# A graph network on one Trainium2 core: the first half of x requested when both edge arrays have landed

## What is computed

```
agg = segment_sum(x[src], dst, N)                       # neighbours of every node
h   = relu(batch_norm(((1 + eps) * x + agg) @ W1 + b1))  # 512 -> 1024
h   = relu(batch_norm(h @ W2 + b2))                      # 1024 -> 512
x   = layernorm(x + x + h)
h   = relu(x @ LW1 + lb1) @ LW2 + lb2                    # 512 -> 256 -> 512
x   = layernorm(x + h + segment_sum(h[src], dst, N))
```

## Time and profile before

| | us |
|---|---|
| median of three runs (lowest, highest) | 286.44 (284.9, 287.74) |
| the profiled execution's own time | 287.6 |
| its span, first to last instruction | 285.8 |
| PE busy | 259.5 (91%) |
| VectorE busy | 144.4 (51%) |
| ScalarE busy | 123.0 (43%) |
| GpSimd busy | 76.6 (27%) |

### The profile page before, as it was taken

One profiled execution on the slowest core, in us unless ns is written; L12 is line 12 of the kernel. 1 busy time (PEld: TensorE's weight loads), 2 busy tenths in 40 slices (PEclk: granted clock), 3 DMA queues, 4 the chain that ended last, 5 costly groups with the idle time before them and its releaser, 6 DMA issues.

```text
span 285.8 us, 4044 instructions
## 1 busy us (share of the span) xinstructions
PE 259.5 (91%) x1581; PEld 221.6 (78%) x1581; DVE 144.4 (51%) x348; ACT 123.0 (43%) x217; POOL 76.6 (27%) x73
## 2 busy tenths in 40 slices
PE   0657999998999999999999999999769999999991
PEld 0636998886888888888888888888649888888770
DVE  1588997552743144444443313004474545448884
ACT  1407353424867047555556220200445445342694
POOL 5420000000920006565656700048301211112120
PEclk9999999999999999999999999999986999999998
DMA  4276000000056810000003795009000000000044
GB/s 139 93 277 240 0 2 0 2 0 6 2 203 236 274 42 1 2 0 0 2 20 126 254 234 102 0 19 202 11 1 2 1 0 2 0 0 2 3 180 175
DMA packets 21846, 20.43 MB, mean 71 GB/s; under 512 B 13911, under 2 KB 14846, under 8 KB 21826
## 3 DMA queue, kind: packets, MB, share of 16 engines
q1 hardware_dynamic: 21320, 19.91, 22.8%
q0 software_dynamic: 160, 0.13, 0.2%
q10 hardware_dynamic: 346, 0.10, 0.2%
HBM read 10.94 MB, written 5.92 MB: 59 GB/s over the span
## 4 chain that ended last, share of the span: by engine, by line
PE 81%; DVE 7%; ACT 5%; DMA 4%; issue 1%; DVEq 0%; SPq 0%; POOLq 0%
PE ps L1006 19%; PE ps L993 19%; PE ps L941 17%; PE ps L1078 7%; PE ps L1067 6%; PE ps L893 3%; PE ps L923 2%; PE ps L1052 2%; DVE hot_s L683 2%; PE ps L1125 2%; DMA src_i<-in_src 2%; PE ps L1043 1%; DMA pairs<-pair 1%; DMA run<-pairs,start_i 1%; PE ps L1064 1%
## 5 line engine op out<-in xcount | busy, mean ns | idle before, releaser
L758 DVE BATCH_NORM_STATS2 stats<-ps 128x6 f32<-128x500 f32 (+1 forms) x36 | 21.6, 599 | 63.1 <-PE ps L1006 35.2
L941 PE MATMUL ps<-AT,xh 128*128 128x500 f32 (+1 forms) x120 | 45.2, 385 | 0.0
L941 PE MATMUL ps<-AT,xl 128*128 128x500 f32 (+1 forms) x120 | 42.8, 364 | 0.0
L993 PE MATMUL ps<-h0h,wh 128*128 128x500 f32 (+1 forms) x96 | 34.0, 354 | 0.0
L993 PE MATMUL ps<-h0h,wl 128*128 128x500 f32 (+1 forms) x96 | 33.8, 352 | 0.0
L993 PE MATMUL ps<-h0l,wh 128*128 128x500 f32 (+1 forms) x96 | 33.7, 351 | 0.0
L443 ACT ACTIVATE AT<-ps 128x500 fp32r<-128x500 f32 x25 | 14.8, 590 | 32.3 <-PE ps L923 32.3
L941 PEld LDWEIGHTS ps<-AT,xl 128*128 128x128 f32 x120 | 24.3, 202 | 2.5
L941 PEld LDWEIGHTS ps<-AT,xh 128*128 128x128 f32 x120 | 24.2, 202 | 2.5
L1006 PE MATMUL ps<-a1h,wl 128*128 128x500 f32 (+1 forms) x96 | 24.9, 354 | 0.0
L1006 PE MATMUL ps<-a1l,wh 128*128 128x500 f32 (+1 forms) x96 | 24.8, 354 | 0.0
(11 more groups left out here) (141 smaller groups left out, 528.8 us busy)
## 6 DMA issues: line engine op xcount, KB each, us to landing
turns<-half_out SPq DMA_DIRECT2D x10, 320.0 KB, 2.2
xs<-in_x SPq DMA_DIRECT2D x1, 2304.0 KB
out<-xs SPq DMA_DIRECT2D x9, 256.0 KB
w1s<-in_L_gnn_W SPq DMA_DIRECT2D x1, 2048.0 KB, 10.4
w2s<-in_L_gnn_W SPq DMA_DIRECT2D x1, 2048.0 KB, 8.3
xs<-in_x SPq DMA_DIRECT2D x1, 1280.0 KB, 7.9
xs<-in_x SPq DMA_DIRECT2D x1, 1024.0 KB
lws<-in_L_gnn_W SPq DMA_DIRECT2D x1, 512.0 KB, 3.6
```

The lines of the kernel that those rows point to most:

```text
L758: link(nc.vector.bn_stats(stats[:, 6 * c:6 * c + 6], ps[:, zbank(t, c), 0:c1 - c0]))
L941: last = mm(o, part[0:r, k, d * P:d * P + P], AT[0:r, k, c0:c1], start=False, stop=(k == NT - 1 and j == 1), skip_group_check=True)
L993: last = mm(ps[:, zbank(t, c), 0:c1 - c0], w[:, t, d * P:d * P + P], h[c][:, d, :], start=(d == 0 and j == 0), stop=(d == DT - 1 and j == 2))
```

## The change

SP waits for both edge arrays before it requests the first half of x. The order of its requests stays; nothing is added or taken away on the other engines.

```
             sp.dma_start(dst_i[0:ER, :], dst.rearrange("(p f) -> p f", p=ER)).then_inc(dst_in, 16)
             sp.dma_start(src_i[0:ER, :], src.rearrange("(p f) -> p f", p=ER)).then_inc(src_in, 16)
+            sp.wait_ge(dst_in, 16)
+            sp.wait_ge(src_in, 16)
             sp.dma_start(xs[:, 0:half, :], x[0:half * P, :].rearrange("(t p) d -> p t d", p=P)).then_inc(x_in, 16)
             sp.wait_ge(lb1_zero, 1)
```

## The result

| | before | changed |
|---|---|---|
| median of 22 runs each, us | 285.88 | 287.47 |
| lowest to highest | 284.08 to 288.44 | 286.04 to 289.84 |
| ratio of the changed kernel to before | | 1.0062, 95% interval 1.0037 to 1.0087 |
| the profiled execution's time (span) | 287.6 (285.8) | 286.79 (284.9) |

The ratio is +1.8 us (+1.1 to +2.5) of 285.88; the medians alone are 1.6 us apart. The forecast was +2.0 us, and 288.4 us on a median of before that then stood at 286.44.

The account below looks back on a forecast made before the run. TensorE's work bounds the kernel, its start set by transfers and VectorE until 28.68 us. +2.2 for the pairs and -0.2 for the sources give +2.0 us on the median 286.44: 288.4 us, range 285.0 to 289.4 for 8 in 10.

Parts of the forecast that it names:

- x's lateness costs nothing: At x's users: x lands at 10.6 to 11.4 us or up to 0.9 later, ahead of 12.15, so no cost.
- The sources: Start of the chain: edge arrays without x behind them, sources land 0.2 us earlier, 0 to 0.45 possible.
- The later x: First half of x: issued at about 5.55 us, 4.0 later, and leaves the engines at 10.5, at most 11.25.
- The slow start: First packets of x below full rate: a loss of 0.7 us, taken between 0.55 and 1.45.
- The pairs: Store of the packed pairs ahead of the first gather: lands at 12.1 us, 2.2 later, up to 2.9.
- the wait for all of x: At the DMA queues: the pairs start only when x has left, at 10.5 us, and land 1.6 us later.
- the rival: At the DMA queues: the pairs get a turn within x, shift -0.3 to +0.9 us, 286.7 us; chance 0.22.
- the 0.8 us that I had added for sharing: Pairs getting a turn within x: landing up to 0.8 us later where they share engines with x.
- The clock: TensorE's fall to 1.2 GHz at 213 to 219 us may differ: median 1.5 to 3 us off; chance 0.10.
- the shift at `rel`: First `rel`, at 14.75 us before: +2.0 us later, carried one for one to the end.

Follow-up runs that it names:

- a1: First half of x requested only when the store of the pairs has landed, against the changed kernel's earlier request; ratio to before 1.0005 (0.9974 to 1.0037).
- a2: x issued by ACT right behind the store of the pairs in the same queue, against SP's request in the changed kernel; ratio to before 0.9984.
- c1: SP waits for the packed pairs in place of the changed kernel's two edge arrays, so x and pairs are requested together; ratio to before 1.0012.
- a3: The changed kernel without the second added wait, so SP waits for the destinations only; ratio to before 1.0021 (0.9987 to 1.0056).
- b2: The changed kernel with only three of x's five tiles requested behind the two waits, the other two once the pairs landed; one run, 286.09 us.
- c2: The kernel before with both edge arrays' loads cut in 112 and 13 rows, x unwaited; ratio to before 1.0023 (0.9985 to 1.0061).
- a4: The kernel before with only three tiles of x requested early, two more once the pairs landed; ratio to before 0.9916 (0.9865 to 0.9967).
- b6: a4 with both edge arrays' loads and the store of the pairs cut in 112 and 13 rows; ratio to before 0.9873 (0.9817 to 0.9928).

## Why the prediction was right, and where only its number was

**Right, and shown.** The wait makes the kernel slower through the store of the pairs, x's lateness costs nothing, and the shift passes on to TensorE's stage: +1.54 at `rel`, +1.51 at the sums. a1, a2 and c1 take the delay of the pairs away by taking x from ahead of them (landing at 7.6 to 8.8), at the price of a later x that then binds; a3 and b2 make it smaller by x's lead and amount, and in c2 the landing stays where x puts it.

**The sources: too small.** Expected 0.2 us earlier, at most 0.45. They came 0.64 earlier, and the destinations 0.62 (4.02 against 4.64). The step that failed is the bound: I took the destinations' time as untouched since x stands behind them in the queue. But x did not stay behind them: from 2.4 to 4.4 us q1 moved 190 packets with 0.19 MB in the kernel before, and the arrays' rows of 680 bytes alone would be 0.13 MB, so rows of x moved among them. In the seven kernels whose first x request comes at 3.98 us or later the destinations are converted at 3.90 to 4.02, and in those with it at 1.51 at 4.64 to 4.86.

**The later x: too fast.** The slow start was to cost 0.7 us, at most 1.45, and x to leave the engines 4.95 us after its request. In the changed kernel its last row was through at 11.2, 6.3 us after it, so 1.3 us of the sum were missing; the request itself came 0.6 us earlier than I had put it. Part of the 1.3 us is the pairs' turns: from 10.8 to 11.0 us only 11 packets of x moved, beside 10 of the pairs. In a1, with the pairs out of the way, the first row moved 1.1 us behind the request and the last was through at about 13.2, 5.6 us behind it; less 3.24 us at the full rate this leaves 1.2 us for the slow start. The landing came 0.8 us later still.

**The pairs: the mechanism was a mixture.** I took the wait for all of x and called a start at 8 to 9 us the rival's sign. They started at 8.65, the rival's sign, and landed at 11.8 us, where the forecast had 11.9 and the rival 9.5 to 11.1. The rival was wrong in the pace: beside x the packets took 2.7 us in place of 1.0, more than the 0.8 us that I had added for sharing. Two errors met, a start too early for my mechanism and an x too slow for my sum: had the pairs waited for x's real end at 11.2, they would have landed at 12.8. That the number was right is partly luck, and the rival deserved more than 0.22. The Trainium skill, page "DMA: Bandwidth & Descriptors", section "Queues, rings and completion order", with its turns between queues packet by packet, describes what happened from 8.65 on better than my reading of the earlier trace rows did. The trace agrees with it only in that there are turns: they were of one row each (45 rows of the pairs in 1 us on five engines), where the page has some 9 to 17 descriptors. What it would not give either is 20 of x's 40 rows an engine ahead of the first turn in the changed kernel, and all 40 in a3.

**The gather: not in the sum.** It took 3.41 us in place of 3.81, since its issue took 1.41 us in place of 1.82. The twelve profiles have 1.40 to 1.91 us for this issue, and VectorE's work at the same time does not explain it: in a4 the subtractions lie over it at 1.40 us, in b6 at 1.91. It stays open, and with 0.4 us it made the forecast of the shift at `rel` (+2.0) miss by 0.5.

**The clock** was rightly kept as a rival beside the sum, but its first low stretch was not seen. The 22 runs average over both stretches; that they cost both kernels the same on average is not shown.

## What to carry to other kernels

A request that nobody waits for can still cost: ask whose small transfer will find it in the DMA engines' queues, and compare the two moments of issue to tenths of a microsecond, since 0.4 us of lead or none (changed, c1) moved the landing by 3.0 us here. Just before the small transfer was the worst of the places tried for the big one. Cut it so that what is needed first goes early and the rest goes behind the small one (a4: the sums 0.9 us earlier), and give small transfers row counts that use more engines (all of it together, b6: 2.0 us earlier, ratio 0.9873). Where the profile names one releaser for a wait on several semaphores, look in the program which of them the instruction waits for. A stretch bound by a landing is judged by the start of the next stage in the trace, and by many runs, where the clock's rises and falls move one execution by up to 3 us.

## What the runs showed of the hardware

- Two transfers of different queues, the small one on five engines: with x requested 1.3 us ahead or more (before, a3), all of its 1.31 MB but 0.1 passed before the pairs moved; with 0.4 us (changed, b2), some 0.7 MB; with none (c1), only 14 packets in the pairs' first 0.8 us. What sets these amounts is not shown.
- From then on the two took turns row for row: 45 rows of the pairs in 1 us on five engines, beside 165 of x on all.
- A store of 125 rows of 680 bytes lands 2.32 us after its issue alone and 6.49 us after it beside x.
- A first row moved 1.1 us behind the request in the changed kernel (6.0 and 4.92) and in a1, and x moved at 80 GB/s from 5.8 to 7.2 us before it came to 395.
- A transfer of 1280 KB took 6.4 us when requested alone at 7.6 us, and 6.2 to 8.0 us in the kernels where it came first or shared engines.
- The first `rel` takes 0.65 to 0.95 us behind a wait and 0.28 us when VectorE comes from other work.
